# Where the context products stand in a half sub-step of a two-layer attention kernel

## Chip, cores and metric

One core of a Trainium2 chip runs the whole program in one launch. The metric is the device time of one execution in microseconds (us); lower is better.

## The reference, cut to what matters

Two layers over 4 sequences of 512 tokens, 256 features. Layer 0 is a linear attention with a per-token low-rank update; layer 1 is a softmax attention with 16 heads of 16 features, then a mixture of 8 small experts. Every one of the four parts is followed by a residual sum and a layer norm.

```python
x = layernorm(x + L0_attn(x)); x = layernorm(x + L0_ffn(x))
# L1 attention
logits = einsum('bhqd,bhkd->bhqk', q, k) / sqrt(16)
ctx = einsum('bhqk,bhkd->bhqd', softmax(logits), v)
x = layernorm(x + (ctx @ Wo + bo))
# L1 experts: router logits, top 2 of 8, silu(gate) * up, down, plus a LoRA branch
x = layernorm(x + L1_ffn(x))
```

In the kernel's order of data the 512 tokens of one "batch" b (0 to 3) are attended within the batch, 16 heads, scores of 512 x 512 a head.

## The kernel before, in words

All engines run programs written out by hand, which meet through semaphores. A first part (`layer0_attention`) takes the span up to about 340 us; small pieces of the later layers for batch 0 stand beside its end. Then comes a short stretch with scores of batch 0 alone, and from 386 us to 715 us the loop that the change touches: `for b in range(B): body(b)` on each of TensorE (PE), ScalarE (ACT), VectorE (DVE), GpSimd (POOL) and SyncE (SP). A tail for batch 3 alone follows.

A batch has 16 sub-steps s (`SUBS`), sub-step s = 4g + kt for head group g (4 heads) and key tile kt (128 keys). Each sub-step is two half sub-steps, n = 2s and 2s + 1, so n goes from 0 to 31. In each half PE issues, in this order:

- `pair(b, n)`: two turned scores (L1134, keys on partitions, 50 rows of the array, into two banks `bank_st` in turn) and beside them two plain scores of 8 heads further on (L1113, 48 rows, into two banks `bank_s` in turn). ACT takes each turned score through exp into one of 8 slots of `probs` (L1460; the trace calls that memory `shared`), DVE takes each plain score through a maximum (L1699, `nmax`). A turned score waits until exp has read the score two before it, a plain score until the maximum of the one two before it is taken. The maxima become the shifts of later exps (`turn_max` L1120, ACT L1465, a DMA by SP).
- in even halves, `context(b, n // 2 - 1)` (L1147): the products of the previous sub-step's four exp tiles with v, 8 instructions in four column strips of 32 into `bank_c`. It waits for the four exps, and at a group's first tile until ACT has copied out `bank_c`.
- one piece of other work for a neighbouring batch, at most one per half. They share the two banks `side`. In even halves of the batches:

```text
n=2  expert_out(b-2)  L1237    n=4  out_project(b-1) L1166   n=6  turn_x2(b+1)   L1033
n=8  query_key(b+1)   L1082    n=10 turn_x3(b-1)     L1033   n=12 value(b+1)     L1096
n=14 query_key(b+1)   L1082    n=16 turn_x1(b+2)     L1033   n=18 select(b+2)    L1047
n=20,22,24,26 expert_up(b-1) L1206 (n=16,18,20,22 in batch 3)  n=28 turn_hm(b+2) L1055
n=30 turn_hidden(b-1) L1226 (n=26 in batch 3)   n=28 expert_out(b-1) in batch 3 alone
```

- after the piece, in a few halves, a turn of maxima or of a finished context (`turn_max`, `turn_context` L1155), `route`, or `turn_logits`.

Each piece first waits for its inputs and for its `side` bank. `query_key(b+1, 0)` at n=8 waits for `x2T_lo` of both halves, which DVE writes at its n=7 (L1686) behind that half's maxima; `turn_x3` at n=10 waits for ACT's normalization of `xk` (L1412, its n=9); `value` at n=12 takes the bank that DVE's `x3T_rest` (L1730, its n=11) reads last; `expert_up` takes the bank that DVE's `weighted_up` (L1743) or, at n=20, `projections` (L1625) reads last.

ACT in half n issues the two exps, then what belongs to the half: at n=8 `qk_out` and then `context_out(b, 0)` (L1470, `bank_c` to `ctT`); at n=16 `context_out(b, 1)` and then `x1T_out` (L1417); at n=24 `context_out(b, 2)`. ACT's exp for sub-step s waits for the context products of s - 2, which free the slots.

In halves where n is 0 the context of the previous batch's last sub-step stands in front of the piece, before and after the change.

Of the kernel before, what the change touches and what calls it, by code (L numbers as in the profile page):

```python
# [80 lines left out]
def at_least(eng, sem, value):  # L81

    if not isinstance(value, int) or value > 0:
        eng.wait_ge(sem, value)
# [641 lines left out]
def update_attention_experts(nc, a, kept, out, first):  # L726
# [6 lines left out]
    with ExitStack() as ctx:  # L733
# [115 lines left out]
        def expert_half(b):  # L849

            return 20 if b + 1 < B else 16
# [167 lines left out]
        def _(pe):  # L1019
# [16 lines left out]
            def turn_x1(b, i):  # L1036
                turn(xf, x1T_done, x1_ready, b, i, selection(b, i))
                last_read[selection(b, i)] = (x1T_ready, 2 * b + i + 1)
# [20 lines left out]
            def update(b, i):  # L1059
                pe.wait_ge(hmT_ready, b + 1)  # L1060
                take(i)
                for t in range(2):
                    tok = (2 * i + t) * P
                    mm = pe.matmul(side_t[i][:, t, :], hmT[:, tok:tok + P], down0[:, :], start=True, stop=True)
                mm.then_inc(up_done, 1)
                last_read[i] = (r2_ready, NT * b + 2 * i + 2)

            def turn_x2(b, i):
                turn(xf, x2T_done, x_ready[2], b, i, i)
                last_read[i] = (x2T_lo_ready, 2 * b + i + 1)  # L1070
# [66 lines left out]
            def context(b, s):  # L1137

                g, kt = divmod(s, 4)
                if s == 0:  # L1140
                    pe.wait_ge(v_ready, 2 * (b + 1))
                    pe.wait_ge(v_ones_ready, 1)
                if kt == 0:
                    at_least(pe, ct_ready, 4 * b + g)
                pe.wait_ge(p_ready, 64 * b + 4 * s + 4)
                for j in range(4):
                    mm = pe.matmul(bank_c[32 * j:32 * j + 32, :], v[:, b % 2, kt, 4 * g + j, :], probs[:, (4 * s + j) % SLOTS, :],  # L1147
                                   start=kt == 0, stop=kt == 3)
                mm.then_inc(pv_done, 1)
# [9 lines left out]
            def out_project(b, c):  # L1159

                pe.wait_ge(cx_ready, 4 * (b + 1))
                pe.wait_ge(wo_in, 16)
                take(c)
                for half_ in range(2):
                    for i in range(2):
                        mm = pe.matmul(side_t[c][:, half_, :], cx[:, 2 * half_ + i, c * P:(c + 1) * P], wo[:, i, :], start=i == 0, stop=i == 1)  # L1166
                mm.then_inc(wo_done, 1)
                last_read[c] = (r3_ready, 2 * b + c + 1)
# [10 lines left out]
            def turn_x3(b, i):  # L1179
                turn(xk[:, b % 2], x3T_done, x_ready[3], b, i, i)  # L1180
                last_read[i] = (x3T_lo_ready, 2 * b + i + 1)
# [48 lines left out]
            def expert_out(b, i):  # L1230
                pe.wait_ge(down1_in, 16)
                pe.wait_ge(hidT_ready, 3 * (b + 1))
                take(i)
                for t in range(2):
                    tok = (2 * i + t) * P
                    for c in range(3):
                        mm = pe.matmul(side_t[i][:, t, :], hidT[:, c, tok:tok + P], down1[:, c, :], start=c == 0, stop=c == 2)  # L1237
                mm.then_inc(down_done, 1)
                last_read[i] = (r4_ready, 2 * b + i + 1)
# [8 lines left out]
            def pair(b, n):  # L1248

                for j in ((2, 3) if n % 2 else (0, 1)):  # L1250
                    turned_score(b, n // 2, j)
                    for batch, u in scores_beside(b, n, j):
                        score(batch, u // 4, u % 4)

            def body(b):
                more, most, back, back2 = b + 1 < B, b + 2 < B, b > 0, b > 1
                e = expert_half(b)
                for n in range(2 * SUBS):
                    pair(b, n)
                    if n % 2 == 0 and n:  # L1260
                        context(b, n // 2 - 1)
                    elif n == 0 and back:
                        context(b - 1, SUBS - 1)

                    if n < 2 and more:
                        update(b + 1, n)
                    if n in (2, 3) and back2:
                        expert_out(b - 2, n - 2)
                    if n in (4, 5) and back:
                        out_project(b - 1, n - 4)  # L1270
                    if n in (6, 7) and more:
                        turn_x2(b + 1, n - 6)
                    if n in (8, 9) and more:
                        query_key(b + 1, n - 8)
                    if n in (10, 11) and back:
                        turn_x3(b - 1, n - 10)
                    if n in (12, 13) and more:
                        value(b + 1, n - 12)
                    if n in (14, 15) and more:
                        query_key(b + 1, n - 12)  # L1280
                    if n in (16, 17) and most:
                        turn_x1(b + 2, n - 16)
                    if n in (18, 19) and most:
                        select(b + 2, n - 18)
                    if n in (e, e + 2, e + 4, e + 6) and back:
                        expert_up(b - 1, (n - e) // 2)
                    if n in (e + 1, e + 3, e + 5, e + 7) and back:
                        expert_gate(b - 1, (n - e) // 2)
                    if n == 28 and most:
                        turn_hm(b + 2)  # L1290
                    if n in (e + 9, e + 10, e + 11) and back:
                        turn_hidden(b - 1, n - e - 9)
                    if n in (28, 29) and not more:
                        expert_out(b - 1, n - 28)

                    if n == 1 and back:
                        turn_context(b - 1, 3)
                    if n == 4:
                        turn_max(b, 1)
                    if n in (9, 17, 25):  # L1300
                        turn_context(b, n // 8 - 1)
                    if n in (11, 19):
                        turn_max(b, n // 8 + 1)
                    if n == 13 and back:
                        route(b - 1)
                    if n == (15 if more else 14) and back:
                        turn_logits(b - 1)
                    if n == 27 and more:
                        turn_max(b + 1, 0)
# [75 lines left out]
            for b in range(B):  # L1385
                body(b)
# [704 lines left out]
```

## Time and profile before

| | us |
|---|---|
| device time, median of 3 runs | 769.73 (767.15 to 775.13) |
| the profiled execution, its own time | 768.48 |
| its span, first to last instruction | 766.7 |
| between the two, outside the span | 1.8 |
| mean granted TensorE clock in the span | 0.934 of full |

Rows of the timeline read: start in us from the span's start, duration in us, engine, line of the kernel, operation, output<-inputs, shape, count of merged instructions, and in brackets how long the engine sat idle just before, and for what. PE is TensorE's matmul side. Matmuls are pipelined, so a matmul's duration reaches into its follower's; the distance between starts is what one costs.

### The profile page before, as it was taken

To read this page: it belongs to the slowest core of one execution; us is meant where nothing else is said; L and a number is where in the kernel's file an instruction comes from. 1 tells how busy PE (TensorE), PEld (TensorE's weight loads), DVE (VectorE), ACT (ScalarE), POOL (GpSimd) and SP (SyncE) were. 2 spreads that over 40 slices of the span, in tenths; PEclk is the share of its full clock that TensorE was granted. 3 is DMA by queue.
4 is the path that set the end of the run, shared out by engine and by line. 5 is a ranking of instruction groups with operands and counts; after the bars stand their busy time and mean duration, and the time that the engine had idled before them with its cause. 6 is when DMAs were issued, how large, how long until landed. Compare 5 with 4: busy or idle time off the path is not lost.

```text
span 766.7 us, 11317 instructions
## 1 busy us (share of the span) xinstructions
PE 700.3 (91%) x4028; PEld 481.7 (63%) x4028; DVE 509.6 (66%) x1125; ACT 405.0 (53%) x746; POOL 110.4 (14%) x107
## 2 busy tenths in 40 slices
PE   4799999999999999997899988999999899999674
PEld 3677988798878887895344534555565455455463
DVE  2657755775577666767778777868779786772343
ACT  2376536643674377453037745764647565656222
POOL 0401321132203322243002010200001000000000
PEclk9899999999999999998559969998999999999868
DMA  8300000010000020008704810373006700000000
GB/s 340 128 0 2 28 1 1 2 31 14 0 0 0 11 77 1 4 1 103 100 2 55 98 15 2 44 90 36 2 2 77 89 30 2 1 2 29 28 1 27
DMA packets 13596, 28.30 MB, mean 37 GB/s; under 512 B 2596, under 2 KB 3436, under 8 KB 13036
## 3 DMA queue, kind: packets, MB, share of 16 engines
q1 hardware_dynamic: 13548, 27.68, 19.6%
q8 instruction: 28, 0.46, 0.3%
q14 instruction: 20, 0.16, 0.1%
HBM read 12.60 MB, written 2.10 MB: 19 GB/s over the span
## 4 chain that ended last, share of the span: by engine, by line
PE 74%; DVE 14%; ACT 5%; issue 3%; DMA 2%; POOL 1%; ACTq 0%; DVEq 0%; POOLq 0%
PE bank_y L391 11%; PE bank_q L332 10%; PE bank_st L1134 9%; PE bank_c L1147 6%; PE bank_a L296 6%; DVE nmax L1699 5%; PE side L1206 4%; PE bank_a L362 3%; PE side L1082 3%; PE bank_s L1113 3%; PE side L1237 2%; PE bank_a L308 2%; PE bank_n L347 2%; PE bank_q L374 2%; PE side L1166 2%
## 5 line engine op out<-in xcount | busy, mean ns | idle before, releaser
L1699 DVE TENSOR_REDUCE nmax<-bank_s 128x1 f32<-128x512 f32 x256 | 164.5, 684 | 62.8 <-PE bank_s L1113 62.2
L1460 ACT ACTIVATE shared<-bank_st 128x512 f32<-128x512 f32 x256 | 139.2, 596 | 78.4 <-PE bank_st L1134 77.8
L1113 PE MATMUL bank_s<-ks,qs 48*128 48x512 f32 x256 | 117.7, 524 | 10.4 <-DVE nmax L1699 8.6
L1134 PE MATMUL bank_st<-qs,ks 50*128 50x512 f32 x256 | 104.8, 480 | 5.6 <-ACT shared L1460 5.4
L578 DVE SCALAR_TENSOR_TENSOR sq<-bank_q,bq,eq 128x512 f32<-128x512 f32 x64 | 47.6, 743 | 52.2 <-ACT eq L473 52.2
L1134 PEld LDWEIGHTS bank_st<-qs,ks 50*128 50x128 f32 x256 | 42.6, 197 | 54.6 <-issue 28.0
L391 PE MATMUL bank_y<-m_hi,s_lo 128*128 128x256 f32 x256 | 73.3, 286 | 3.2 <-POOL s_lo L248 3.1
L1147 PE MATMUL bank_c<-shared,v 128*32 128x512 f32 x512 | 73.5, 648 | 0.9 <-ACT shared L1460 0.9
L391 PE MATMUL bank_y<-m_lo,s_hi 128*128 128x256 f32 x256 | 72.1, 282 | 0.0
L391 PE MATMUL bank_y<-m_hi,s_hi 128*128 128x256 f32 x256 | 72.1, 282 | 0.0
L248 POOL TENSOR_TENSOR s_lo<-sq,s_hi 128x512 fp32r<-128x512 f32 x32 | 42.8, 1339 | 189.5 <-ACT s_hi L478 189.5
L1113 PEld LDWEIGHTS bank_s<-ks,qs 48*128 48x128 f32 x256 | 47.4, 208 | 30.1 <-DVE nmax L1699 27.4
L478 ACT ACTIVATE s_hi<-sq 128x512 fp32r<-128x512 f32 x64 | 40.3, 631 | 44.1 <-DVE sq L595 44.1
L471 ACT ACTIVATE eq<-bank_q,bq_neg 128x512 f32<-128x512 f32 x64 | 43.9, 685 | 33.9 <-PE bank_q L332 33.1
L595 DVE TENSOR_TENSOR sq<-sq,bank_q 128x512 f32<-128x512 f32 x64 | 43.4, 683 | 23.5 <-PE bank_q L374 23.2
L332 PE MATMUL bank_q<-xT_hi,wq_lo 128*128 128x512 f32 x128 | 54.6, 427 | 1.3 <-DVE sq L578 1.3
L957 POOL TENSOR_TENSOR ln_rstd<-ln_var,half 128x4 f32<-128x4 f32 x12 | 12.1, 1012 | 285.0 <-DVE ln_var L118 285.0
L391 PEld LDWEIGHTS bank_y<-m_hi,s_lo 128*128 128x128 f32 x256 | 48.2, 188 | 5.8 <-issue 3.0
L332 PE MATMUL bank_q<-xT_hi,wq_hi 128*128 128x512 f32 x128 | 50.5, 394 | 0.0
L332 PE MATMUL bank_q<-xT_lo,wq_hi 128*128 128x512 f32 x128 | 50.4, 394 | 0.0
L391 PEld LDWEIGHTS bank_y<-m_lo,s_hi 128*128 128x128 f32 x256 | 48.2, 188 | 0.2
L391 PEld LDWEIGHTS bank_y<-m_hi,s_hi 128*128 128x128 f32 x256 | 48.2, 188 | 0.0
(251 smaller groups left out, 1329.8 us busy)
## 6 DMA issues: line engine op xcount, KB each, us to landing
qs<-qk_hi SPq DMA_DIRECT2D x16, 256.0 KB, 5.9
ks<-qk_hi SPq DMA_DIRECT2D x16, 256.0 KB, 10.2
xT<-in_xT SPq DMA_DIRECT2D x4, 512.0 KB, 5.3
sq<-in_wqT SPq DMA_DIRECT2D x2, 1024.0 KB, 9.2
wo<-in_woT SPq DMA_DIRECT2D x1, 2048.0 KB, 12.9
xs<-in_x SPq DMA_DIRECT2D x1, 2048.0 KB, 17.8
qs<-qk_lo SPq DMA_DIRECT2D x8, 256.0 KB, 7.9
ks<-qk_lo SPq DMA_DIRECT2D x8, 256.0 KB, 10.9
```

The lines of the kernel that those rows point to most:

```text
L248: pool.tensor_tensor(s_lo[:, n % 3, :], sq[:, n, :], s_hi[:, n % 3, :].bitcast(F32), ALU.subtract).then_inc(s_lo_ready[1], 1)
L296: mm = pe.matmul(bank[:, :], lhs, rhs, start=n == 0, stop=n == 3 * KD - 1)
L332: mm = pe.matmul(q_bank("query", n)[:, :], lhs, rhs, start=i == 0, stop=i == 3 * KD - 1)
L391: mm = pe.matmul(bank_y4[:, t, :], lhs, rhs, start=n == 0 and i == 0 and t % 2 == 0, stop=n == H0 - 1 and i == 2, skip_group_check=True)
L471: act.activation(eq[:, n % 3, :], q_bank("query", n)[:, :], ACT.Relu, bias=bq_neg[:, h:h + 1], scale=-1.0).then_inc(eq_capped, 1)
L578: dve.scalar_tensor_tensor(out=sq[:, n, :], in0=q_bank("query", n)[:, :], scalar=bq1[:, h:h + 1], in1=eq[:, n % 3, :], op0=ALU.add, op1=AL ...
L595: dve.tensor_tensor(sq[:, n, :], sq[:, n, :], q_bank("factor", n)[:, :], ALU.mult).then_inc(scaled, 1)
L1113: pe.matmul(bank_s[u % 2][:, :], qs[part, b % 2, slot, t * P:(t + 1) * P], ks[part, b % 2, slot, :], start=True, stop=True).then_inc(s_don ...
L1134: pe.matmul(bank_st[u % 2][:, :], ks[part, b % 2, slot, kt * P:(kt + 1) * P], qs[part, b % 2, slot, :], start=True, stop=True).then_inc(st ...
L1147: mm = pe.matmul(bank_c[32 * j:32 * j + 32, :], v[:, b % 2, kt, 4 * g + j, :], probs[:, (4 * s + j) % SLOTS, :], start=kt == 0, stop=kt == 3)
L1460: act.activation(probs[:, u % SLOTS, :], bank_st[u % 2][:, :], ACT.Exp, scale=SCALE1).then_inc(p_ready, 1)
L1699: dve.tensor_reduce(nmax[:, g, t, j:j + 1], bank_s[u % 2][:, :], AX.X, ALU.max, negate=True).then_inc(max_ready, 1)
```

## The change

In an even half with n > 0, `context(b, n // 2 - 1)` is issued behind the half's piece (and still ahead of the turns that follow the piece), not ahead of it. Nothing else is changed: the same instructions, the same waits inside each, the same order on ACT, DVE, POOL and SP.

```diff
@@ tensor body(b), loop over n @@
                     pair(b, n)
-                    if n % 2 == 0 and n:
-                        context(b, n // 2 - 1)
-                    elif n == 0 and back:
+                    if n == 0 and back:
                         context(b - 1, SUBS - 1)
-
                     if n < 2 and more:
                         update(b + 1, n)
...
                     if n in (28, 29) and not more:
                         expert_out(b - 1, n - 28)
 
+
+                    if n % 2 == 0 and n:
+                        context(b, n // 2 - 1)
                     if n == 1 and back:
                         turn_context(b - 1, 3)
                     if n == 4:
```

## Rows read from the trace of the kernel before

**Rows 1.** The page, part 1: busy time of TensorE.

```profile
PE 700.3 (91%) x4028; PEld 481.7 (63%) x4028; DVE 509.6 (66%) x1125; ACT 405.0 (53%) x746; POOL 110.4 (14%) x107
```

**Rows 2.** The page, part 4: the chain that ended last, by engine.

```profile
PE 74%; DVE 14%; ACT 5%; issue 3%; DMA 2%; POOL 1%; ACTq 0%; DVEq 0%; POOLq 0%
```

**Rows 3.** Waits of PE, 386 to 722 us: total us, times, longest.

```profile
PE bank_st L1134 <- ACT shared L1460: 5.4, 12, 0.7
PE bank_s L1113 <- DVE nmax L1699: 5.2, 5, 1.8
...
PE side L1082 <- DVE x2T_lo L1686: 0.8, 2, 0.4
```

**Rows 4.** Timeline, batch 1, half 8, and the next pair.

```profile
487.19 1.07 PE L1147 MATMUL bank_c<-shared,v 128*32 128x512 f32 x8
487.28 1.27 DVE L1686 TENSOR_TENSOR x2T_lo<-side,x2T_hi 128x512 fp32r<-128x512 f32 x2
...
488.65 0.47 PE L1082 MATMUL side<-x2T_hi,wqkv_lo 128*128 128x512 f32 x1 [0.40 <-DVE x2T_lo L1686]
...
490.20 0.50 PE L1134 MATMUL bank_st<-qs,ks 50*128 50x512 f32 x1
...
490.54 0.39 PE L1134 MATMUL bank_st<-qs,ks 50*128 50x512 f32 x1
```

**Rows 5.** Timeline, batch 0, half 8.

```profile
408.38 1.28 DVE L1686 TENSOR_TENSOR x2T_lo<-side,x2T_hi 128x512 fp32r<-128x512 f32 x2
...
408.95 1.06 PE L1147 MATMUL bank_c<-shared,v 128*32 128x512 f32 x8
...
409.94 0.50 PE L1082 MATMUL side<-x2T_hi,wqkv_lo 128*128 128x512 f32 x1
```

**Rows 6.** Timeline, batch 1, half 10, and the next pair.

```profile
493.07 2.06 ACT L1412 ACTIVATE xk<-xk,ln_shift,ln_rstd 128x256 f32<-128x256 f32 x4
...
493.58 1.07 PE L1147 MATMUL bank_c<-shared,v 128*32 128x512 f32 x8
...
494.57 0.66 PE L1033 MATMUL side<-ident,xk 128*128 128x128 f32 x4
...
495.67 0.50 PE L1134 MATMUL bank_st<-qs,ks 50*128 50x512 f32 x1 [0.44 <-ACT shared L1460]
```

**Rows 7.** Timeline, batch 1, half 12.

```profile
498.06 0.68 DVE L1730 TENSOR_TENSOR x3T_lo<-side,x3T_hi 128x512 fp32r<-128x512 f32 x1
...
498.63 1.06 PE L1147 MATMUL bank_c<-shared,v 128*32 128x512 f32 x8
```

**Rows 8.** Timeline, batch 0, ACT behind half 16, and the pair of half 18.

```profile
431.60 0.60 ACT L1470 ACTIVATE ctT<-bank_c 128x512 f32<-128x512 f32 x1
...
432.15 0.60 ACT L1417 ACTIVATE x1T<-side 128x512 f32<-128x512 f32 x1
...
432.65 1.08 ACT L1460 ACTIVATE shared<-bank_st 128x512 f32<-128x512 f32 x2
...
433.74 0.50 PE L1134 MATMUL bank_st<-qs,ks 50*128 50x512 f32 x1
```

**Rows 9.** Timeline, batch 1, halves 20 to 22.

```profile
523.15 0.39 PE L1206 MATMUL side<-win_hi,x3T_lo 128*128 128x256 f32 x1 [0.62 <-DVE pr L1625]
...
527.58 0.49 PE L1113 MATMUL bank_s<-ks,qs 48*128 48x512 f32 x1 [1.06 <-DVE nmax L1699]
```

**Rows 10.** Timeline, batch 1, half 26: a bank freed and the context.

```profile
539.68 0.41 DVE L1743 TENSOR_TENSOR uw<-side,rt_wh 128x256 f32<-128x256 f32 x1
...
540.92 1.07 PE L1147 MATMUL bank_c<-shared,v 128*32 128x512 f32 x8
```

**Rows 11.** Three windows: busy us of each engine, then PEclk, the granted clock.

```profile
444.20:457.90 13.70, 13.30 (x51) 4.76 (x49) 9.45 (x27) 5.66 (x11) 2.03 (x5) 0.50 0.00 0
...
529.50:536.40 6.90, 6.90 (x28) 4.33 (x28) 5.18 (x18) 2.44 (x5) 0.64 (x3) 0.51 0.01 2
...
611.40:614.90 3.50, 3.50 (x16) 1.74 (x10) 2.19 (x8) 0.96 (x2) 0.00 (x0) 0.51 0.58 65
```

## The prediction

> **What bounds the kernel now.** I read the page first: TensorE is busy 91% of the span [rows 1] and the chain that ended last lies on it for 74%, on VectorE for 14%, on ScalarE for 5% [rows 2]. That is an average over stages, so next came the waits of PE inside the loop that the change touches. From 386 to 722 us PE stands still for other engines for little: 5.4 us for exps and 5.2 us for maxima, both at the scores, and 0.8 us in two waits of 0.4 at L1082 [rows 3]. So the loop is bound by PE's own order nearly everywhere: what PE does is paid in full, and a wait that it gains is paid in full as well, unless PE would have stood for the same engine a little later.
>
> Then the timeline, half by half. For every even half two times count: C, when the pair is out and the next thing can start (now the start of the context products), and R, when the piece's inputs and bank are ready. Now the piece starts at C plus the context's length, or at R if that is later. In batch 1, half 8, the context starts at 487.19; DVE's two x2T_lo end at 487.28 + 1.27 = 488.55; the piece starts at 488.65 after a wait of 0.40 [rows 4]. So the context takes 488.65 - 0.40 - 487.19, about 1.0 us (0.99 in batch 0: 408.95 to 409.94 [rows 5]), and it lies in the shadow of a VectorE chain that PE has to wait for anyway. A semaphore takes about 0.1 us from DVE's end to PE's start.
>
> **The change part by part.** It moves 42 of the context blocks behind a piece (7 in batch 0, 14, 12 and 9 in batches 1 to 3); where an even half has no piece, nothing moves. No instruction is added or removed on any engine, no DMA and no queue order of SP or POOL changes.
>
> *The context's own waits.* It needs the four exps of the sub-step before; the second turned score of the same half waits for just these, so it never waits longer than the pair did, in either place. The slots that it frees are asked for by ACT one half sub-step later than its new place: nothing there.
>
> *PE's order.* With R before C the half is as long as before: 1.0 us context plus piece, in either order. With R after C, the context no longer fills the gap, and the half grows by R - C, at most by the context's 1.0. The list over the 42:
>
> - Half 8, batch 1: R = 488.65, C = 487.19; 1.46 apart, so +1.0, the whole cap. PE stands 1.46 us where it stood 0.40 [rows 4]. Batch 2 has the other of the two waits of 0.4 [rows 3]: +1.0.
> - Half 8, batch 0: x2T_lo ends at 408.38 + 1.28 = 409.66, R = 409.76, C = 408.95 [rows 5]: +0.81.
> - Half 10, batches 1 to 3: two tiles of xk are ready half way through the four (493.07 + 1.03 = 494.10, R = 494.2), C = 493.58: the half grows by 0.6. But the next pair starts only at 495.67, after 0.44 of waiting for an exp [rows 6] that stands behind that same normalization on ACT. Piece from 494.2 (0.6 long), context to 495.8: 0.1 late for the first score, and not for the second, which waits for the second exp. I take 0 (ends: 0 and 0.6, three times).
> - Half 12, batch 1: the bank comes free at 498.06 + 0.68 = 498.74, R = 498.84, C = 498.63 [rows 7]: +0.21, and I count batch 2's twin the same: 0.4 together.
> - Half 20, batch 1: the piece starts at 523.15 after a wait of 0.62 for DVE [rows 9]; without the context in front it waits 1.6, and context and next pair come 1.0 later. But two halves on PE waits 1.06 for a maximum until 527.58 [rows 9], and DVE's row of small work before that does not depend on PE's order. That wait takes up the 1.0: 0.
> - The rest (31 halves, and two with under 0.4 that ScalarE's next exp or the tail's rounding covers): R is before C. Typical is half 26 of batch 1: the bank is free at 539.68 + 0.41 = 540.09, C is 540.92 [rows 10]. That cover of 0.8 is the thing to know: if DVE falls back by more, these halves begin to pay too. 0.
>
> *ScalarE's order.* In halves 16 and 24 ACT's next thing behind the exps is the copy of bank_c, which now becomes ready a piece later. In half 16 of batches 0 and 1 the x1T copy stands behind it. Now ctT starts at 431.60, x1T at 432.15, the exps of half 17 at 432.65, and the pair of half 18 at 433.74 [rows 8]. With the piece (0.6 us) ahead of the context, ctT starts some 0.55 later, and so do the exps: 433.20 to 434.28. The first score of the pair needs the first exp (433.75, in time within 0.1), the second, due 0.33 later (as 490.20 and 490.54 in [rows 4]) at 434.07, needs the second at 434.3: +0.3, twice, 0.6. In half 24 no second copy stands behind it and the odd piece covers it: 0. In half 8 the reverse holds: the qk copy runs beside the context now and ACT is about 0.5 freer, but the pair of half 10 does not wait there: 0. Ends for all of this: from -0.5 to +1.0.
>
> *Switching on the array.* Each half now goes pair, piece, context, pair. A context straight behind a full-width piece never occurs in the trace of before, so its price is bounded: a context after a pair starts 0.3 us after the last score does, and the start of a pair after a piece shows the same distance within about 0.05. Over 42 halves that is -2 to +2 us. I take 0, as the nearest rows differ by nothing.
>
> Sum: 1.0 + 1.0 + 0.8 + 0.4 + 0.6 = 3.8 us. From the profiled execution's 768.48 (766.7 of span and 1.8 outside) that gives 772.3. The median of the runs is 769.73, 1.25 above the profiled one; since it is the median that will be compared, I forecast 769.73 + 3.8 = **773.5 us**, 0.5% slower. A measurement here tells about 1% (7.7 us) from no change, so this counts as the same.
>
> **The rivals.**
>
> *A: the longer waits cost clock (slower).* TensorE's granted clock falls to about half (1.2 of 2.4 GHz) in three stretches of the loop: 13.7, 6.9 and 3.5 us long [rows 11]. The middle one begins 2 us after PE stood 1.06 us for a maximum [rows 9]. Since PE is busy through these stretches, one of length T costs up to T/2. After the change PE stands about 1.5 us in one go at half 8 of batches 1 and 2, and 1.6 us at half 20. Against it: at half 8 dense full-width products follow at once. If each of the two gets one stretch like the shortest or the middle one, +1.75 to +3.45 each: 773.5 + 3.5 = 777.0, at most 780.4.
> The Trainium skill, page "TensorE: Matmul & The Clock Gate", section "A second HAM failure mode: psum-queue depth-cycling", says that frequent short idles between groups of matmuls make the clock fall and recover in turns. By that rule this change goes wrong through the clock rather than by the 3.8 us of waits; the trace agrees in so far as the stretch in batch 1 follows two waits, 0.62 and 1.06 [rows 9, 11].
>
> *B: the clock gains (faster).* The same rows the other way round. At half 20 to 22 of batch 1 the wait of 1.06 disappears into the one at the piece. If the 6.9 us stretch does not come then, up to 3.45 are saved; if a shift of a few us also moves the 3.5 us one away, 1.75 more. From two of the three stretches on this decides: 773.5 - 5.2 = 768.3, and with half of the 13.7 us one too, 764.9. Against it: the idle sum there is the same, and the pairs and context products around it too.
>
> *C: it is absorbed (no change).* The +1.0 of half 8 could vanish in later waits: in batch 1 the 0.44 at half 11 [rows 6] and the 1.06 [rows 9]. Against: the first hangs on ACT work that follows PE's query_key itself, and DVE waits for PE again between the two, so both shift along. If still half goes: 771.6. That the change buys something by giving ACT and DVE the piece's result 1.0 us earlier belongs here: the 10.6 us of waits for exps and maxima [rows 3] mostly stand behind odd halves, whose order is as it was. With 1 us from it as well: 770.6.
>
> *D: more halves pay.* If DVE and ACT lag by more than the 0.8 us of cover [rows 10] after the shifts, each expert_up half pays up to 0.3. Ten such: 776.5.
>
> **How the numbers follow.** Forecast 0.50 (771.5 to 775.5), A 0.17, B 0.09, C 0.14, D 0.10. The range 768.5 to 779.0 holds the forecast, C, D, most of A and the near half of B. The runs of before lie 8 us apart, which a median of a few shares, so I keep it that wide. Faster by over 1% (under 762.0) needs all three clock stretches and luck: 0.03. Slower by over 1% (over 777.4) is the far half of A and of D and a high median: 0.16. The rest, 0.81, is within 1%.
>
> **What would show it.** In the timeline after: L1082 in half 8 of batches 1 and 2 starts with a wait of about 1.4 us for x2T_lo, and the context follows it; the total wait of L1082 on L1686 goes from 0.8 to about 3.6 in three waits. In half 20 of batch 1 the wait for pr is about 1.6, and the 1.06 for nmax is nearly gone. In half 10 L1033 waits about 0.6 for xk, and the exp wait after it shrinks from 0.44 to about 0.3. In half 16 ctT starts behind the last context product. The granted clock's mean stays within 0.01 of 0.934. I am wrong if L1082's waits are as now, if the loop's length (386 to 715 us) doesn't grow by 3 to 5 us at equal clock, or if piece-then-context starts show a step above 0.4 us between the last product of the one and the first of the other.

## The result, and the profile after

| | before | after |
|---|---|---|
| median of the timed runs, us | 770.49 (766.71 to 779.62, 20 runs) | 778.63 (776.82 to 785.22, 20 runs) |
| ratio, with its 95% interval | | 1.010 (1.0071 to 1.0128) |
| the profiled execution, its own time | 768.48 | 776.98 |
| its span | 766.7 | 775.1 |
| mean granted TensorE clock | 0.934 | 0.931 |

The change costs 8.1 us between the medians, 1.0%. The forecast was 773.5, with a range up to 779.0: the time lies in the range, 0.4 us below its upper end, and just beyond "slower by over 1%", which the forecast had given 0.16. It lies outside the 771.5 to 775.5 of the forecast itself, and nearer to rival A's 777.0. Of the 8 us the forecast's sum explains less than half; that the range holds the rest is owed to its width. The ratios given below are those of the records, which need not be the quotients of the medians.

The page of the kernel after, part 1, busy time by engine, and part 4, the chain that ended last (they answer to [rows 1, 2]):

```profile
PE 703.9 (91%) x4028; PEld 480.8 (62%) x4028; DVE 507.5 (65%) x1125; ACT 406.4 (52%) x746; POOL 110.3 (14%) x107
...
PE 73%; DVE 16%; ACT 4%; issue 3%; DMA 2%; POOL 1%; ACTq 0%; DVEq 0%; POOLq 0%
```

The work is the same, 4028 instructions. PE is busy 3.6 us longer for them, so not all of the new time is waiting: part of it is products that ran slower. The chain has moved from PE (74 to 73%) to DVE (14 to 16%), as a wait that PE gained would show.

Waits of PE in the loop, 386 to 730 us, kernel after (total us, times, longest; answers to [rows 3]):

```profile
PE bank_s L1113 <- DVE nmax L1699: 4.2, 4, 1.8
PE bank_st L1134 <- ACT shared L1460: 3.8, 9, 0.5
PE side L1082 <- DVE x2T_lo L1686: 3.5, 3, 1.4
PE side L1033 <- ACT xk L1412: 1.9, 3, 0.8
```

L1082 now waits three times for 3.5 us (0.8 before; about 3.6 in three was forecast). The waits for maxima fell by 1.0 us and those for exps by 1.6. The 1.9 at L1033 is new: it is half 10, where the waits for exps became smaller.

Half 8 of batch 1, kernel after, timeline (answers to [rows 4]):

```profile
491.44 0.68 DVE L1686 TENSOR_TENSOR x2T_lo<-side,x2T_hi 128x512 fp32r<-128x512 f32 x1
...
492.82 0.47 PE L1082 MATMUL side<-x2T_hi,wqkv_lo 128*128 128x512 f32 x1 [1.40 <-DVE x2T_lo L1686]
...
494.19 0.63 PE L1082 MATMUL side<-x2T_hi,wqkv_hi 128*128 128x512 f32 x1
...
494.75 1.93 PE L1147 MATMUL bank_c<-shared,v 128*32 128x512 f32 x8
...
496.61 0.79 PE L1134 MATMUL bank_st<-qs,ks 50*128 50x512 f32 x1
```

PE stands 1.40 us where it stood 0.40, and the context comes behind the piece. But its eight instructions now take 1.93 us where they took 1.07, and the next pair starts 1.86 after them (1.0 when the clock is full). They have the same shape and wait for nothing. Windows of the kernel after (busy time of each engine, then PEclk, the granted clock as a share of full; they answer to [rows 11]):

```profile
445.95:463.00 17.05, 16.70 (x68) 6.24 (x64) 10.44 (x29) 8.34 (x16) 2.03 (x5) 0.50 0.00 1
476.70:483.50 6.80, 6.70 (x21) 3.12 (x20) 3.41 (x12) 0.60 (x1) 1.21 (x2) 0.51 0.00 1
493.70:497.20 3.50, 3.50 (x14) 1.06 (x14) 0.77 (x6) 1.05 (x2) 2.51 (x3) 0.52 0.11 22
582.50:585.90 3.40, 2.70 (x6) 1.82 (x6) 2.35 (x8) 0.00 (x0) 0.91 (x1) 0.52 0.00 0
616.60:623.40 6.80, 6.68 (x23) 3.39 (x24) 4.45 (x15) 2.66 (x6) 0.00 (x0) 0.51 0.35 38
```

The third and the fourth stretch at the lower level (1.2 GHz) begin at the wait of half 8, in batches 1 and 2. The third begins 1.1 us behind the wait's end, the fourth at 582.6, while PE still stands: its wait of 1.40 ends at 583.20. Neither was there before.

```profile
583.20 0.76 PE L1082 MATMUL side<-x2T_hi,wqkv_lo 128*128 128x512 f32 x1 [1.40 <-DVE x2T_lo L1686]
```

The first is longer (17.1 for 13.7), the second is new, the one of [rows 11] at 529.50 is gone. The prediction speaks of three stretches of the loop before; there is a fourth, which begins ahead of the loop at 362.3 and reaches 17 us into it. Window of the kernel before:

```profile
386.00:403.20 17.20, 16.94 (x53) 6.91 (x53) 11.75 (x28) 6.49 (x12) 1.23 (x2) 0.50 0.01 1
```

With it, between the first and the last pair of the loop, the stretches sum to 40.8 us before and 53.7 after. Between these pairs lie 327.3 and 336.2 us: the loop grew by 8.8. The context products above took 1.86 times as long at the lower level. If all work did, the 12.9 us more at that level cost 12.9 x (1 - 1/1.86), some 6.0: an estimate of the clock's part in this one execution, which leaves 2.9 for the order.

To see where the 8 us arise, I compared the start of every pair in the two traces. "Step" below means by how much the lag of one kernel behind another grows from one half to the next.

| lag of after behind before | us |
|---|---|
| loop's start | -0.8 |
| batch 0, half 20 | 0.0 |
| batch 1, half 0 (behind the stretch now 17.1 us long) | +1.0 |
| batch 1, half 5 (in the new stretch at 476.7) | +4.2 |
| batch 1, half 9 (behind half 8: a step of 2.3) | +6.4 |
| batch 1, half 20 | +6.6 |
| batch 1, half 26 (the stretch at 529.5 is gone) | +4.4 |
| batch 2, half 9 (again a step of 2.3) | +6.8 |
| end of the loop | +8.0 |

### The profile page after: what moved, and what is told of

The parts are those of the page before. It is cut to its first block, busy times and chain, and to the rows that moved or that the text cites. A ratio compares the mean times of both kernels' runs of the same rounds, so it can differ in the third digit from the quotient of the medians.

```text
span 775.1 us, 11317 instructions
## 1 busy us (share of the span) xinstructions
PE 703.9 (91%) x4028; PEld 480.8 (62%) x4028; DVE 507.5 (65%) x1125; ACT 406.4 (52%) x746; POOL 110.3 (14%) x107
## 4 chain that ended last, share of the span: by engine, by line
PE 73%; DVE 16%; ACT 4%; issue 3%; DMA 2%; POOL 1%; ACTq 0%; DVEq 0%; POOLq 0%
PE bank_y L391 10%; PE bank_q L332 10%; PE bank_st L1134 8%; PE bank_c L1147 7%; DVE nmax L1699 6%; PE bank_a L296 5%; PE side L1206 3%; PE side L1082 3%; PE bank_s L1113 3%; PE bank_a L362 3%; PE side L1237 2%; PE bank_a L308 2%; PE side L1166 2%; PE bank_n L347 2%; PE bank_q L374 2%
## 5 line engine op out<-in xcount | busy, mean ns | idle before, releaser
L1147 PE MATMUL bank_c<-shared,v 128*32 128x512 f32 x512 | 75.1, 662 | 0.9 <-ACT shared L1460 0.9
```

## The experiments

There are twelve kernels. The ratios compare each with the kernel before on the same chip and in the same job. Beside the medians I use one more number. A run lists its span and its mean clock, so its time at the lower level is about 2 x (1 - clock) x span: 2 x 0.066 x 766.7 = 101 us in the profiled execution of before. Over all timed runs but two (one of before with 860.45 us, one of e6 with 1261.57), inside each kernel, the time rises by 0.34 us for each us of that (0.015 either way). With it a difference can be read "at equal clock", that is, without what the clock happened to do. It is a regression, and not a measurement of any one stretch.

In the expectations K stands for "waits cost clock", W for "waits alone" and S for "a price per moved block".

### Half 8 alone, all but half 8, half 8 filled, half 20 alone

The first two take the change apart, on the kernel before (`behind` says in which half the context stands behind the piece: n == 8 in e1_only8, n != 8 in e2_not8, n == 20 in e4_only20):

```diff
-                    if n % 2 == 0 and n:
+                    behind = n == 8
+                    if n % 2 == 0 and n and not behind:
                         context(b, n // 2 - 1)
...
+                    if n % 2 == 0 and n and behind:
+                        context(b, n // 2 - 1)
```

e1_only8, half 8 alone:

> The kernel before with the move in half 8 alone. Theory W+K (the longer waits cost themselves and then clock): +2.8 us of waits (1.0, 1.0, 0.8) and one stretch at half clock behind the wait of 1.4 in batches 1 and 2, so +5 to +6 against before, more than half of the whole change's +8. Theory W (waits alone, the rest of the +8 comes from elsewhere, such as a switching cost per moved block): +2.8. Theory S (the price is per moved block, 42 of them at 0.2): +0.6 for 3 blocks plus 2.8 of waits, 3.4.

Measured: 774.40 against 770.48, ratio 1.0037 (1.0003 to 1.0070). Three waits at L1082 with the same sum, by this row of PE's waits:

```profile
PE side L1082 <- DVE x2T_lo L1689: 3.5, 3, 1.4
```

The clock fell at half 8 in batches 0 (409.6 to 413.0) and 1 (491.5 to 495.0), both times before the wait had ended, and not in batch 2. By the means of the runs the kernel is 2.8 ± 1.5 us slower than before: less than the 5 to 6 that W+K had expected, and what W and S had. The steps of its order sum to 2.1: 0.8, 1.0 and 1.0 at half 8, less 0.35 at half 12 of batches 1 and 2.

e2_not8, the whole change but half 8:

> The changed kernel with half 8 put back, the other 39 blocks moved. W+K: it loses the 2.8 of waits and the clock behind them, so +2 to +3 against before is left. W: +5 (8.1 less 2.8). S: 39 x 0.2 = +7.8 less nothing of the waits, so about +5 to +8.

Measured: 772.12, ratio 1.0029 (0.9992 to 1.0067), and the wait as before the change:

```profile
PE side L1082 <- DVE x2T_lo L1689: 0.8, 2, 0.4
```

The clock fell behind no half 8. Against the changed kernel this is 778.6 - 772.1 = 6.5 us by medians and 5.6 ± 2.6 by means, against the 2.8 ± 1.5 that half 8 costs alone: half 8 carries a large part of the change, and the two differences do not fix it better than that. Three waits longer by 0.8, 1.0 and 1.0 are 2.9 of it. Against before, +2.4 ± 2.3 fits W+K's 2 to 3 and lies on the edge of W's 5.

e3_fill8 is the change with PE kept at work in the wait: unread full-width products of about 0.23 us each.

```diff
+            def keep_busy(count):
+                take("t")
+                for _ in range(count):
+                    pe.matmul(bank_t[:, :], wqkv_hi[:, 0, 0:P], wqkv_hi[:, 0, 0:T], start=True, stop=True)
...
+                    if n == 8 and more:
+                        keep_busy(3 if b == 0 else 5)
                     if n in (8, 9) and more:
                         query_key(b + 1, n - 8)
```

> The changed kernel, and in half 8, between the pair and the piece, 3 (batch 0) or 5 (batches 1 and 2) full-width matmuls of 512 columns into the bank of the turns that nobody reads, 0.23 us each, which run while PE would wait for x2T_lo. The piece starts no later. W+K: the waits' 2.8 stay but no stretch at half clock begins at half 8 of batches 1 and 2; 2.5 us faster than the changed kernel, +5 to +6 against before. W and S: as the changed kernel, +8, or a little more.

Measured: 775.42, ratio 1.0063 (1.0024 to 1.0102), 3.2 below the changed kernel (3.3 ± 2.0 by the means), as W+K had expected and W and S had not. Timeline of half 8 in batch 1:

```profile
491.65 1.43 PE L1251 MATMUL bank_t<-wqkv_hi 128*128 128x512 f32 x5
491.74 1.27 DVE L1693 TENSOR_TENSOR x2T_lo<-side,x2T_hi 128x512 fp32r<-128x512 f32 x2
...
493.11 0.47 PE L1082 MATMUL side<-x2T_hi,wqkv_lo 128*128 128x512 f32 x1
...
494.67 1.06 PE L1147 MATMUL bank_c<-shared,v 128*32 128x512 f32 x8
495.67 0.49 PE L1134 MATMUL bank_st<-qs,ks 50*128 50x512 f32 x1
```

The piece starts no earlier, since it still has to wait for DVE. But the context takes 1.06 again and the pair follows after 1.0. The steps behind half 8 are 0.79, 1.06 and 1.07 us in batches 0 to 2: the forecast's 0.8, 1.0 and 1.0. At half 8 what remains after filling is the order's price alone; what filling took away there is the clock's. Elsewhere this kernel still has stretches, the one of 6.8 us at 477.1 among them.

e4_only20, half 20 alone:

> The kernel before with the move in half 20 alone (it counts in batches 1 to 3). W+K: the wait for pr grows from 0.6 to 1.6, the wait of 1.06 for the maximum two halves on shrinks by the same; no loss of waits, and the half-clock stretch of batch 1 (6.9 us before) becomes shorter or vanishes, so -3 to 0 against before. W: 0. S: +0.6.

Measured: 769.36, ratio 0.9978 (0.9950 to 1.0006). In its own job that is no gain that can be told; against all runs of before it is a small one, in time at the lower clock and not at equal clock (table below). Its wait is the 1.6 of the kernel after:

```profile
PE side L1206 <- DVE pr L1628: 1.6, 1, 1.6
```

The stretch at 529.5 is gone here too. So the wait of half 20 is absorbed, as forecast. That it costs no clock holds for this trace and for the kernel after, and not in general: nine of the profiled kernels have this wait of 1.6 us in batch 1, and in six of them (e2, e3, e6, e8, e10, e12) a stretch of 3.4 us begins at it. Window of e2_not8, whose wait ends at 529.95:

```profile
530.30:533.70 3.40, 3.40 (x16) 1.45 (x16) 3.16 (x11) 0.00 (x0) 0.00 (x0) 0.50 0.00 1
```

### The halves that should cost nothing

e5_free moves the context in all even halves but 8, 10, 12, 16 and 20. That is 27 of the 42 blocks (the expectation says 31; each of the five halves has a piece in three batches):

```diff
+                    behind = n not in (8, 10, 12, 16, 20)
```

> The move in 31 of the 42 halves alone: all but 8, 10, 12, 16 and 20, that is, where the piece's inputs are there before the pair is out and no copy on ScalarE stands in line. W+K: the order costs nothing, 0 against before within 1, and at equal clock 0 within 0.5. S (a price per moved block): the 2 us that the kernel without the move in half 8 still lost would be here, +1.5 to +2.

Measured: 772.59 (767.55 to 779.24), ratio 1.0018 (0.9977 to 1.0059). Outside the stretches of lower clock the only lasting steps are three of 0.10 us, behind half 4 of batches 1 to 3, where `turn_max` now stands directly behind the context; a step of 0.12 at half 6 of batch 0 is given back a half later. The other halves stay within 0.07 us, which settles the switching of piece and context in this trace: its bounds of -2 to +2 shrink to about 0.3. The runs alone would not settle it: at equal clock they say +1.2 ± 0.5, above the 0.5 that was expected, and below S's 1.5 to 2 by less than the error.

### DVE's work earlier, in the changed kernel

e6_after_dve8 lets DVE write x2T_lo ahead of the sums for the layer norm, so that half 8 waits less:

```diff
+                    if n == 7 and more:
+                        x2T_rest(b + 1, 0)
+                        x2T_rest(b + 1, 1)
                     if n in (6, 7) and back:
...
-                    if n == 7 and more:
-                        x2T_rest(b + 1, 0)
-                        x2T_rest(b + 1, 1)
```

> The changed kernel with VectorE's two x2T_lo ahead of the statistics of the same half 7 (0.7 us in batches 1 and 2). W+K: the waits of 1.4 at L1082 fall to 0.7, so 1.4 us less of waits, and less or no clock lost behind them; 2 to 4 us faster than the changed kernel, +4 to +6 against before. W: 1.4 faster, +6.7. S: no change.

Measured: 777.39, ratio 1.0073 (1.0035 to 1.0111). One of its twelve runs took 1261.57 us, which nothing here explains; the other eleven have a median of 776.45.

```profile
PE side L1082 <- DVE x2T_lo L1686: 2.2, 3, 0.7
```

The waits lost 1.3 us. The steps behind half 8 are 0.84, 1.98 and 0.39: in batch 1 the clock fell again (492.2 to 495.6), though the wait was 0.74. By the median the gain is 2.2 us, with wide error: not enough to tell an effect of the clock from one of the order.

### Filling a wait that was there before

The 13.7 us stretch of [rows 11] begins behind a wait of 1.8 us, which PE has behind half 21 of batch 0, in the next pair. Timeline of the kernel before:

```profile
443.89 0.54 PE L1113 MATMUL bank_s<-ks,qs 48*128 48x512 f32 x1 [1.81 <-DVE nmax L1699]
```

e7_fill21 is the kernel before with eight unread products issued ahead of that pair:

```diff
                     pair(b, n)
...
+                    if b == 0 and n == 21:
+                        keep_busy(8)
```

> The kernel before, with 8 full-width matmuls that nobody reads behind the pair of half 21 of batch 0, where PE stands 1.8 us for a maximum. They fill a wait and move nothing. K (a wait that PE stands idle brings the half clock, and that is worth 0.3 to 0.4 us per us of it): the stretch of 13.7 us behind it shortens or goes, -2 to -5 against before. If waits have nothing to do with the clock: 0.

Measured: 765.76, ratio 0.9942 (0.9905 to 0.9979): 0.6% faster than the kernel before, a small gain but clear of the interval. Timeline and window of e7_fill21:

```profile
440.96 2.13 PE L1251 MATMUL bank_t<-wqkv_hi 128*128 128x512 f32 x8
...
443.77 0.50 PE L1113 MATMUL bank_s<-ks,qs 48*128 48x512 f32 x1 [0.25 <-DVE nmax L1706]
...
443.00:458.00 15.00, 12.91 (x75) 5.22 (x76) 12.92 (x33) 8.96 (x18) 2.03 (x5) 1.00 0.03 4
```

The fillers cover the wait down to 0.25, and the same part of the loop runs at full clock (1.00) where it had 0.50 [rows 11]. Nor is this one trace's luck: in the ten profiled kernels that leave this wait unfilled a stretch of 10 to 20 us begins at it every time, and in the four that fill it (e7, e8, e9, e11) none does.

e8_best adds to e7 the move of half 20 and DVE's reordering of e6_after_dve8:

```diff
+                    behind = n == 20
...
+                    if n == 7 and more:
+                        x2T_rest(b + 1, 0)
+                        x2T_rest(b + 1, 1)
```

> The kernel before with the move in half 20 alone, VectorE's x2T_lo ahead of the statistics in half 7, and the 8 filling matmuls of batch 0. W+K: the gains add, -1.7 for half 20, -0.8 for the two waits of 0.4, -2 to -5 for the filled wait: -4 to -7 against before, faster than both kernels. W: -0.8. S: +0.6 - 0.8, no change.

Measured: 765.63, ratio 0.9942 (0.9911 to 0.9973). Nothing is added to e7's gain. In its trace DVE's reordering shortens half 8 of batches 1 and 2 by 0.45 each, and half 11 takes the same back.

e9_after_fill8_21 is the changed kernel with both fillings, of half 8 and of half 21:

```diff
+                    if b == 0 and n == 21:
+                        keep_busy(8)
...
+                    if n == 8 and more:
+                        keep_busy(3 if b == 0 else 5)
```

> The changed kernel with both fillings: half 8 (3, 5, 5 matmuls) and half 21 of batch 0 (8). Against the kernel before with the filling of half 21 alone (765.8 median, 5.3 us under the kernel before in the mean) only the order of the context differs, with the two large waits filled in both. W+K: what is left between the two is the waits' own price, 4 to 5 us, so 769 to 771, about -1 against before; half 9 starts 0.8, 1.1 and 1.1 later in batches 0, 1 and 2. W: 8 between the two, 773 to 774.

Measured: 775.14, ratio 1.0020 (0.9988 to 1.0053), its mean 8.1 us above e7's. W+K had expected 769 to 771, with 4 to 5 between these two, and was wrong here; W's 8 between them came true. No stretch begins behind a half 8; but there are two in batch 3 that e7 lacks, at 662.2 to 669.0 and 679.2 to 692.9. Its runs spend 99.9 us at the lower clock, e7's 86.9; at equal clock the two differ by 3.8, which is the order's price. So the rest of the 8 is a clock that falls elsewhere, and filling half 8 does not reach it. Whether the new order brings these falls, no run shows.

e11_fill21_b1 is e7 with four more products behind the piece of half 21 in batch 1:

```diff
+                    if b == 1 and n == 21:
+                        keep_busy(4)
```

> The kernel before with the filling of half 21 in batch 0 (8) and one more behind the piece of half 21 in batch 1 (4 matmuls), where PE stands 1.06 us for a maximum and a stretch of 6.9 us at half clock followed. K: that stretch goes too, -1 to -2 against the first filling alone, so -6 to -7.5 against before. If the first filling's gain was chance of where it fell: no better than -5.

Measured: 765.86, ratio 0.9932 (0.9903 to 0.9961), no gain over e7. The two stretches of 3.4 us that e7 has, at 525.5 and 607.4, are gone, and one of 6.8 came at 655.2 to 662.0: the sum is the same. The expected -6 to -7.5 did not come.

### ScalarE's order in half 16

e10_act16 is the changed kernel with the x1T copy ahead of the copy of bank_c:

```diff
+                    if n in (16, 17) and most:
+                        x1T_out(b + 2, n - 16)
                     if n in (8, 16, 24):
...
-                    if n in (16, 17) and most:
-                        x1T_out(b + 2, n - 16)
```

> The changed kernel, ScalarE's x1T copy of half 16 ahead of its copy of bank_c, as the piece is now ready first. If the late exps of half 17 come from that queue, the steps of +0.3 that pair 18 and its followers show in batches 0 and 1 go (0.4 us in all, seen in the timeline; the time of one run cannot show it). If they come from elsewhere they stay.

Measured, a single execution: 770.19, span 768.4. The kernel after, batch 0 (answers to [rows 8]):

```profile
431.87 0.60 ACT L1470 ACTIVATE ctT<-bank_c 128x512 f32<-128x512 f32 x1 [0.70 <-PE bank_c L1147]
432.36 0.59 ACT L1417 ACTIVATE x1T<-side 128x512 f32<-128x512 f32 x1
432.84 1.10 ACT L1460 ACTIVATE shared<-bank_st 128x512 f32<-128x512 f32 x2
...
433.49 0.50 PE L1134 MATMUL bank_st<-qs,ks 50*128 50x512 f32 x1
433.99 0.49 PE L1134 MATMUL bank_st<-qs,ks 50*128 50x512 f32 x1
```

and e10_act16:

```profile
431.14 0.61 ACT L1417 ACTIVATE x1T<-side 128x512 f32<-128x512 f32 x1
431.96 0.60 ACT L1470 ACTIVATE ctT<-bank_c 128x512 f32<-128x512 f32 x1 [0.21 <-PE bank_c L1147]
432.45 1.08 ACT L1460 ACTIVATE shared<-bank_st 128x512 f32<-128x512 f32 x2
433.51 0.50 PE L1134 MATMUL bank_st<-qs,ks 50*128 50x512 f32 x1
433.85 0.39 PE L1134 MATMUL bank_st<-qs,ks 50*128 50x512 f32 x1
```

ACT stood 0.70 for the context while the copy it could make stood behind. Swapped, the exps come 0.4 earlier and the pair's second score starts 0.34 after the first, not 0.50. The steps of 0.08 and 0.25 in batch 0 and of 0.08 and 0.12 in batch 1 are gone. That is about 0.5 us. The 8 us between this execution and the changed kernel's median are something else: in this execution the clock did not fall behind any half 8, though L1082 waited 3.5 us in all as before. The same two places as in the kernel after, windows of e10_act16:

```profile
489.50:493.00 3.50, 3.50 (x22) 1.97 (x22) 2.09 (x5) 2.30 (x5) 3.15 (x3) 1.00 0.44 87
...
579.00:583.00 4.00, 4.00 (x26) 2.13 (x18) 2.54 (x5) 2.91 (x6) 3.58 (x3) 1.00 0.54 94
```

So the wait does not force the fall. One execution can't say whether ACT's order has a part in this.

### The changed kernel once more

e12_again is the changed kernel as it is, for a second profiled execution:

> The changed kernel once more, for its share of half clock and for where the stretches stand in a second trace. If the longer waits of half 8 bring the half clock by themselves, it falls there again in both batches and the mean is 7 to 9 us above before. If it is a matter of how the waits lie to the chip's own time, one or none of the two stands there, as in the run with ScalarE's order changed, while the steps of the waits, 0.8, 1.0 and 1.0 at half 9, are the same whatever the clock does.

Measured: 782.68 over six runs, ratio 1.0133 (1.0081 to 1.0184). The runs fall in two groups, 774.16 and 774.46 at a clock of 0.933, and four of 782.49 to 783.69 with 0.918 or near it. The profiled one is of the second group. Its windows behind half 8 of batches 0, 1 and 2:

```profile
410.40:413.80 3.40, 3.37 (x10) 1.84 (x14) 1.13 (x2) 0.60 (x1) 0.69 (x1) 0.54 0.00 0
492.30:495.80 3.50, 2.64 (x6) 1.82 (x6) 2.50 (x9) 0.00 (x0) 0.85 (x1) 0.54 0.00 0
584.50:587.90 3.40, 3.40 (x15) 0.96 (x15) 0.97 (x6) 0.65 (x2) 2.20 (x3) 0.54 0.00 1
```

Three falls of three, and a mean 8.8 us above before: as expected if the waits bring the falls by themselves, and against e10's none of three. The steps are 2.41, 2.33 and 2.39, where the same halves cost 0.80, 1.04 and 1.06 at full clock (e10): a fall here costs 1.3 to 1.6 us. The kernel also has stretches in batch 3, at 670.1 to 676.9 and 687.2 to 700.8.

### What the twelve say together

Does the clock fall at half 8? A fall is counted where a stretch begins between the wait's start and 1.1 us behind its end, in batches 0, 1 and 2 of each profiled kernel:

| half 8 | profiled kernels | falls |
|---|---|---|
| context behind, wait 0.75 to 1.4 us, not filled | after, e12, e1, e10 | 7 of 12 |
| context behind, wait 0.74 to 0.75, not filled | e6 | 1 of 3 |
| context behind, wait filled | e3, e9 | 0 of 6 |
| context in front, wait at most 0.4 | before, e2, e4, e5, e7, e8, e11 | 0 of 21 |

Of the unfilled waits, those of 1.40 us had a fall in 5 of 8 cases and those of 0.75 in 3 of 7.

Half 8 is not the only such place. The other long waits of PE in the loop, with a fall counted where a stretch begins between the wait's start and 2.5 us behind its end (3.1 in batch 3, whose waits are short):

| wait | in | falls |
|---|---|---|
| batch 0, pair of half 22, 1.8 us, not filled ahead of it | 10 kernels | 10 |
| the same, filled | 4 | 0 |
| batch 2, pair of half 20, 1.26 us | 14 | 11 |
| batch 1, piece of half 20, 1.6 us (context behind) | 9 | 6 |
| batch 1, pair of half 22, 1.06 us (half 20 as before), not filled | 4 | 3 |
| batch 1, pair of half 4, 0.77 us | 14 | 7 |
| batch 0, half 11, 1.0 us | 14 | 1 |
| batch 3, pair of half 8, 0.53 and 0.36 us | 14 | 6 |
| batch 3, pair of half 16, 0.54 us | 14 | 4 |

Of the 59 stretches that begin in the loop in the fourteen traces, 47 begin within 2.5 us of a wait of 0.6 us or more; ten of the other twelve are the ones in batch 3. So a stretch nearly always begins at a wait, and which of the waits get one changes from execution to execution. The shorter waits bring it less often, and the length alone does not decide: the 1.0 us of half 11 had one in 14.

And the means of the timed runs, against all 101 distinct runs of before from the four jobs together (two standard errors behind the sign; "at equal clock" by 0.34 us for each us of time at the lower clock):

| kernel | mean less before's | us at the lower clock | at equal clock |
|---|---|---|---|
| before, 101 runs | | 106.7 ± 1.8 | |
| after, 20 | +8.0 ± 1.4 | 115.8 ± 3.5 | +4.9 ± 0.5 |
| e1, half 8 alone | +2.8 ± 1.5 | 108.9 | +2.0 ± 0.7 |
| e2, all but half 8 | +2.4 ± 2.3 | 109.4 | +1.5 ± 0.7 |
| e3, half 8 filled | +4.7 ± 1.9 | 107.2 ± 5.3 | +4.5 ± 0.7 |
| e4, half 20 alone | -2.1 ± 0.9 | 101.1 | -0.2 ± 0.4 |
| e5, free halves | +1.3 ± 2.6 | 107.0 | +1.2 ± 0.5 |
| e6, change, DVE earlier, 11 runs | +5.8 ± 2.2 | 118.3 | +1.8 ± 0.9 |
| e7, half 21 filled | -5.2 ± 1.8 | 86.9 | +1.5 ± 0.5 |
| e8, half 21 filled, half 20, DVE earlier | -5.1 ± 1.5 | 87.5 | +1.4 ± 0.6 |
| e9, change, both filled | +3.0 ± 1.4 | 99.9 | +5.3 ± 0.7 |
| e11, half 21 filled in batches 0 and 1 | -5.2 ± 1.5 | 89.3 | +0.7 ± 0.8 |
| e12, change again | +8.8 ± 3.8 | 120.4 | +4.1 ± 0.9 |

The change costs 4 to 5 us at equal clock, and some 9 us more at the lower clock, which by the regression are the other 3.

## Why the prediction was right in part, and where it failed

**Half 8, right.** The forecast's 1.0, 1.0 and 0.8 were measured as 1.06, 1.07 and 0.79 with the wait filled. R - C, capped at the context's length, gave the right price here, and the waits (1.4 in batch 1) came out as worked out.

**Half 10, right.** Timeline of the kernel after, batch 1 (answers to [rows 6]):

```profile
499.76 2.07 ACT L1412 ACTIVATE xk<-xk,ln_shift,ln_rstd 128x256 f32<-128x256 f32 x4
...
500.89 0.66 PE L1033 MATMUL side<-ident,xk 128*128 128x128 f32 x4 [0.57 <-ACT xk L1412]
...
501.48 1.07 PE L1147 MATMUL bank_c<-shared,v 128*32 128x512 f32 x8
...
502.47 0.50 PE L1134 MATMUL bank_st<-qs,ks 50*128 50x512 f32 x1
```

The piece waits 0.57 (0.6 forecast), and the wait for an exp that was in front of the next pair is gone (0.44 before, 0.3 forecast): a step of +0.12, then -0.13, sum nothing.

**Half 12, wrong sign.** "+0.21, and I count batch 2's twin the same." Timeline after, batch 1 (answers to [rows 7]):

```profile
504.25 0.68 DVE L1730 TENSOR_TENSOR x3T_lo<-side,x3T_hi 128x512 fp32r<-128x512 f32 x1
504.28 0.50 PE L1134 MATMUL bank_st<-qs,ks 50*128 50x512 f32 x1
...
505.08 0.36 PE L1096 MATMUL side<-wqkv_hi,x2T_lo 128*128 128x256 f32 x1
...
506.66 1.07 PE L1147 MATMUL bank_c<-shared,v 128*32 128x512 f32 x8
507.66 0.49 PE L1134 MATMUL bank_st<-qs,ks 50*128 50x512 f32 x1
```

From pair to pair the half takes 507.66 - 504.28 = 3.38 us; before it took 3.62 (497.62 to 501.24). C came earlier, 0.80 behind the pair's start where it was 1.01, and R came earlier still: DVE frees the bank at 504.93, 0.65 behind the pair's start where it was 1.12. So R no longer lies behind C: -0.24 in each of two batches. The forecast had kept both where they were. Two kernels show what moved them. e2, with half 8 as before, pays +0.23 and +0.24 at half 12, the forecast's size; e1, with half 8 alone moved, gains 0.35 and 0.34 there. So it is the move in half 8 that puts DVE ahead of PE here; the forecast should have asked what it does to the halves behind it.

**Half 16, right in kind, too large.** 0.3 twice was forecast; batch 0 paid 0.33 after a gain of 0.16 a half earlier, batch 1 0.19. e10 shows the mechanism, since with the copies swapped these steps are gone.

**Half 20, right.** Timeline after, batch 1 (answers to [rows 9]):

```profile
529.63 0.38 PE L1206 MATMUL side<-win_hi,x3T_lo 128*128 128x256 f32 x1 [1.62 <-DVE pr L1625]
...
530.53 1.07 PE L1147 MATMUL bank_c<-shared,v 128*32 128x512 f32 x8
531.53 0.49 PE L1134 MATMUL bank_st<-qs,ks 50*128 50x512 f32 x1
...
534.06 0.49 PE L1113 MATMUL bank_s<-ks,qs 48*128 48x512 f32 x1
```

The piece waits 1.62, and the score that waited 1.06 for its maximum shows no wait of its own: +0.87 at first, given back two halves on. From half 20 to half 28 the lag falls by 2.17; in e1, which leaves half 20 as it was and has no stretch there either, it falls by 2.08. So nothing of the 0.87 stays.

**The rest and switching, right within 0.3.** There are three steps of 0.10 at half 4, which the forecast did not have.

The steps of the order sum to about 3.0 us in the trace against the forecast's 3.8. At equal clock the runs say 4.9 ± 0.5, while for e1 and e2 steps (2.1 and about 1.3) and runs (2.0 and 1.5) agree. The two differ by more than their errors, and I can't say by what; a us at the lower clock need not cost the same in every place, which the regression takes for granted. e7 shows it: 20 us less of them saved 5.2 and not 6.8.

**The step that failed: the clock was kept out of the sum.** The forecast gave rival A, "the longer waits cost clock", a chance of 0.17, and set against it that "at half 8 dense full-width products follow at once". That was no protection. The clock fell between 0.6 us ahead of those products' start and 1.1 us behind it in 7 of 12 cases with the longer wait, and in none of 27 where it was at most 0.4 us or filled. (The three cases of one execution may hang together: 3 of 3 in e12, 0 of 3 in e10.) Each fall costs 1.3 to 1.6 us, so on average 7/12 x 3 x 1.3 = 2.3 us of the 8, and 3.9 where all three come. That is less per stretch than A's price (1.75 to 3.45), but in more places: A counted batches 1 and 2, and batch 0 with its wait of 0.75 fell too. Filling took 3.2 us off the median, close to this. At A's other place, half 20, a stretch began in 6 of 9 traces. The forecast had read a stretch behind a wait in its own rows [rows 9, 11] and yet put this term at nothing.

The Trainium skill, page "TensorE: Matmul & The Clock Gate", section "A second HAM failure mode: psum-queue depth-cycling", names frequent short idles between groups of matmuls as what lets the clock fall and recover in turns. The runs agree with its direction, with 7 of 12 against 0 of 27; in them the same wait was sometimes followed by a fall and sometimes by none.

**Rival B's saving came, and its cause is not shown.** The stretch of 6.9 us at 529.5 is missing after the change, which saved about 3.0 us; half 25, whose scores now wait for maxima, took 0.84 of it back. But it is not the wait's going that took it away: e1 kept the wait of 1.06 and has no stretch there, and six kernels without that wait have one of 3.4 us, behind the wait of 1.6 that replaces it. In the profiled execution of the kernel after this was luck. All other kernels lose the same 0.84 at half 25, but e5 (0.58), whether a short stretch or none stands there.

**What stays open.** The 4.2 us that the profiled execution lost up to half 5 of batch 1, 3.2 of them in a new stretch at 476.7, are bound to no edit by any run. The new stretch begins 0.4 us behind a wait of 0.77 us for a maximum that every kernel has, the one before too. A stretch follows it in 7 of 14 traces, five with and two without most of the moved blocks; it is in e2 and in e3, so half 8 and its wait are not needed for it. Nor is the clock in batch 3 bound to an edit: e2, e4, e5, e9, e11 and e12 had stretches there that before had not. Order price (3.0 to 4.9) and half 8's falls (2.3 to 3.9) can make up the 8.0 between them, but a part of this size may as well come from there: e9 stays 8.1 above e7 with half 8 filled, 4.4 of it by the regression from the lower clock.

## What to carry to other kernels

Work that waits for nothing belongs in front of work that has to wait, and what a swap costs can be read half by half as the distance from "could start" to "inputs ready", capped by the length of the moved work. Recompute both after every earlier shift: half 12 changed its sign by what half 8 did. Where TensorE sets the time, a wait of about 1 us can cost more than itself: list all such waits, look at the granted clock at and behind each, and price the chance of a fall there. Take that chance from several traces, since one trace of the same kernel showed 2 falls of 3 and another 3 of 3. A wait that can't be covered by real work may be worth filling with unread products: here eight of them took 5 us, 0.6%, off the kernel before, more than any reordering tried.

## What of the hardware was unexpected

- Unread products in a 1.8 us wait kept the clock at full for the 15 us behind it, where it had been half for 13.7 us; with them no stretch began there in 4 traces of 4, without them in none of 10 did it stay away.
- The granted clock can fall while PE still stands: in four of the seven falls at half 8 the stretch begins before the wait has ended, by 0.2 to 0.6 us.
- The same kernel has executions at 774 and at 783 us on one chip in one job (e12), with mean clocks of 0.933 and 0.918. Repeating the profile showed what one profile couldn't: 2 falls of 3 behind half 8 in one, 3 of 3 in the other.
- A stretch at the lower clock that is removed in one place often comes back in another (e11: the ones at 525.5 and 607.4 gone, one at 655.2 new, time unchanged), so that the sum of removed stretches is no forecast of the gain.
- Eight context instructions in four column strips cost 1.0 us in all at full clock and 1.86 at the lower level, nearly the same ratio as for full-width products (0.23 and 0.43 us from start to start at L1082). Behind a full-width piece they start without a step that could be measured.
